# 480-column product blocks and a wider low matmul in a float32r AdaLN/LoRA feed-forward kernel

## The reference, cut to what matters

```python
# x: (8, 256, 1024) float32, ids: (8,) adapter numbers
y      = einsum('bsi,boi->bso', x, weight[ids])              # adapter, 1024 -> 1024
base   = y @ base_W.T + base_b                               # 1024 -> 1024
probs  = softmax(y @ router_W.T + router_b)                  # 15 routes
w      = sum over the 8 highest probs, by expert_map         # gate of each of 8 experts
h      = einsum('btd,erd->bter', y, A)                       # 8 experts x rank 16 = 128
out    = x + base + 2.0 * einsum('bter,eor->bto', h * w[..., None], B)
```

## Time and profile before

| | us |
|---|---|
| median of 3 runs | 404.02 |
| lowest, highest | 403.29, 405.07 |
| the profiled execution | 402.98 |
| its span, first to last instruction | 401.2 |

### The profile page before, as it was taken

One profiled execution on the slowest core, in us unless ns is written; L12 is line 12 of the kernel. 1 busy time (PEld: TensorE's weight loads), 2 busy tenths in 40 slices (PEclk: granted clock), 3 DMA queues, 4 the chain that ended last, 5 costly groups with the idle time before them and its releaser, 6 DMA issues.

```text
span 401.2 us, 5972 instructions
## 1 busy us (share of the span) xinstructions
PE 394.9 (98%) x2102; PEld 348.5 (87%) x2102; DVE 301.0 (75%) x561; ACT 157.7 (39%) x223; POOL 6.0 (1%) x13
## 2 busy tenths in 40 slices
PE   7999999999999999999999999999999999999996
PEld 6888888888888888889888888888888888888985
DVE  2769988878979884788758896589856899468763
ACT  3667344572145511554025630365304643144300
POOL 0000210000000000000000000000000000000000
PEclk9999999999999999999999999999999999999999
DMA  7999697830267305563066520775026830464002
GB/s 286 401 391 399 116 203 236 305 107 0 105 261 263 105 0 207 176 244 105 0 221 239 203 70 11 258 268 191 3 79 234 306 113 0 137 230 158 2 0 105
DMA packets 27277, 67.56 MB, mean 168 GB/s; under 512 B 3458, under 2 KB 14210, under 8 KB 27266
## 3 DMA queue, kind: packets, MB, share of 16 engines
q1 hardware_dynamic: 25106, 62.47, 43.9%
q0 software_dynamic: 1872, 3.90, 4.9%
q10 hardware_dynamic: 288, 1.05, 0.8%
HBM read 58.08 MB, written 8.39 MB: 166 GB/s over the span
## 4 chain that ended last, share of the span: by engine, by line
PE 93%; DMA 2%; DVE 2%; issue 1%; SPq 1%; ACT 0%; DVEq 0%
PE y_ps L823 27%; PE y_ps L825 14%; PE pl_ps L848 7%; PE x_ps L859 6%; PE x_ps L858 6%; PE x_ps L860 6%; PE s_ps L859 5%; PE s_ps L860 5%; PE s_ps L858 5%; PE pl_ps L849 4%; DMA w_raw<-in_wT 2%; PE y_ps L836 2%; PE s_ps L873 1%; PE s_ps L875 1%; PE s_ps L874 1%
## 5 line engine op out<-in xcount | busy, mean ns | idle before, releaser
L823 PE MATMUL y_ps<-x_split,w_hi 128*128 128x512 f32 x496 | 173.6, 394 | 0.3 <-DVE y_sum L529 0.3
L825 PE MATMUL y_ps<-x_split,w_lo 128*128 128x256 f32 x496 | 139.0, 280 | 0.0
L823 PEld LDWEIGHTS y_ps<-x_split,w_hi 128*128 128x128 f32 x496 | 92.9, 187 | 21.7 <-DVE w_lo L511 0.6
L825 PEld LDWEIGHTS y_ps<-x_split,w_lo 128*128 128x128 f32 x496 | 93.7, 189 | 0.4
L388 ACT CAST w_hi<-w_raw 128x1024 fp32r<-128x1024 f32 x58 | 60.8, 1049 | 75.8 <-DMA w_raw<-in_wT 75.5
L511 DVE TENSOR_TENSOR w_lo<-w_raw,w_hi 128x1024 fp32r<-128x1024 f32 x58 | 70.9, 1224 | 18.5 <-ACT w_hi L388 17.0
L380 ACT COPY y_sum<-y_ps 128x256 f32<-128x256 f32 x62 | 23.2, 374 | 66.6 <-PE y_ps L825 66.5
L848 PE MATMUL pl_ps<-pl_split,y_hi 128*128 128x480 f32 x128 | 42.7, 383 | 0.0
L529 DVE TENSOR_TENSOR y_sum<-y_ps,y_sum 128x256 f32<-128x256 f32 x62 | 26.1, 421 | 16.5 <-ACT y_sum L380 16.5
L849 PE MATMUL pl_ps<-pl_split,y_lo 128*128 128x240 f32 x128 | 34.9, 273 | 0.0
L858 PE MATMUL s_ps<-st_hi,y_hi 128*128 128x464 f32 x80 | 30.4, 380 | 0.0
(11 more groups left out here) (112 smaller groups left out, 543.3 us busy)
## 6 DMA issues: line engine op xcount, KB each, us to landing
w_raw<-in_wT SPq DMA_DIRECT2D x60, 512.0 KB, 3.4
res<-in_x SPq DMA_DIRECT2D x16, 512.0 KB, 4.7
x_raw<-in_xT SPq DMA_DIRECT2D x14, 512.0 KB, 4.8
out<-res SPq DMA_DIRECT2D x13, 512.0 KB, 3.4
early_raw<-in_wT SPq DMA_DIRECT2D x4, 512.0 KB, 8.5
hi_raw<-in_base_t SPq DMA_DIRECT2D x2, 928.0 KB, 10.5
st_raw<-in_base_t SPq DMA_DIRECT2D x2, 928.0 KB, 12.3
st_raw<-in_base_t POOLq DMA_DIRECT2D x2, 928.0 KB, 9.3
```

The costliest lines, as they stand in the source:

```text
L823: nc.tensor.matmul(y_ps[:, c % 2, :], w_hi[:, s, k, :], x_split[:, k, :, :].rearrange("p s t -> p (s t)"), start=(k == 0), stop=False)
L825: mm = nc.tensor.matmul(y_ps[:, c % 2, 0:T], w_lo[:, s, k, :], x_split[:, k, 0, :], start=False, stop=(k == KC - 1))
```

## The change

The number of plain columns goes from 96 to 64. With it NH goes from 464 to 480, PL from 240 to 208, HALF from 48 to 32, and the tiles that hold them follow. Line 848 becomes 2 x 208 = 416 wide. The low matmul of the plain part (line 849) would be 208 wide; it is made WL = 256 wide: it reads 208 high columns and the first 48 low columns of `pl_split[:, k]`, and so adds the product of the low part of `y` and the low part of the first 48 columns of A where high by low of these columns is summed. That is a term which the kernel before leaves out.

```diff
-    NP = 96
+    NP = 64
     NH = (D - NP) // 2
     PL = AR + NP
     DH = D // 2
     HALF = NP // 2
+    WL = 256
...
                         nc.tensor.matmul(pl_ps[:, t, 0:2 * PL], hi, pl_split[:, k, :, :].rearrange("p s n -> p (s n)"), start=(k == 0), stop=False)
-                        mm = nc.tensor.matmul(pl_ps[:, t, 0:PL], lo, pl_split[:, k, 0, :], start=False, stop=(k == KC - 1))
+                        mm = nc.tensor.matmul(pl_ps[:, t, 0:WL], lo, pl_split[:, k, :, :].rearrange("p s n -> p (s n)")[:, 0:WL],
+                                              start=False, stop=(k == KC - 1))
```

## The result

The changed kernel takes 407.87 us (median of 4 runs, 407.2 to 408.8) where the kernel before takes 403.65 us beside it: ratio 1.011, 95% interval 1.008 to 1.014. A second set of runs of the same changed kernel gave 407.25 against 403.27 us, 1.0096 (1.0079 to 1.0113). It is 4.0 to 4.2 us slower, and the forecast was 402.9 us with a range that ended at 406.8.

The account below looks back on a forecast made before the run. The prediction took the distances between TensorE's matmul starts to bound the kernel. Products +2.1, plain part -3.0, LoRA -0.2 and first stage 0 summed to -1.1 us, giving 402.9 us from a 404.02 us median, range 401.3 to 406.8 us.

Parts of the forecast that it names:

- What bounds the kernel: Whole run: TensorE, 98% busy at 2.4 GHz, sets the time as the sum of distances between 2,100 matmul starts.
- The price of 480: Block products: a 480-wide matmul costs its columns at 2.4 GHz plus 32 clock periods (13.3 ns), 213.3 ns.
- the other reading: Block products: 480 priced from its neighbour 464 with columns added and 3.5 ns kept, 216.9 ns; listed but not taken.
- Products: 684 block-product matmuls going from 464 to 480 columns, 3.1 ns more each: +2.1 us.
- Plain part: 128 pairs going from 480 and 240 to 416 and 256 columns, 23.3 ns less each: -3.0 us.
- LoRA: 96 matmuls of 512 columns, now preceded by a multiple of 32, at most 2.2 ns less each: -0.2 us.
- First stage: Unedited pairs of 512 and 256 columns in each element: 0 us if fast and slow stretches stay where they are.
- the cover that can fail: First stage's rhythm staying put: -0.9 us if the slow rhythm goes, +2.3 us if it spreads to the other 354 pairs.
- Covers: Work beside TensorE, such as conversions and y_lo, stays hidden at no cost; about 0.3 us left for B00 and y_lo.
- My balance of the loads: Transfers: block loads carry 32 KB more each, plain loads 64 KB less each, 128 KB against 128 KB.
- columns alone: Rival: no reward for multiples of 32; products +4.6 us, plain pairs -2.6 us, together +2.0 us, 406.0 us; chance 0.2.
- the spread of the slow rhythm: Rival: slow rhythm in all first stages (+2.3 us) and plain pairs (+0.8 us), total +2.0 us, 406.0 us; chance 0.12.

Follow-up runs that it names:

- the second changed execution: Second profiled execution of the unedited changed kernel, with no wait that the kernel before doesn't have: span 404.8 us, against 401.2 us before.
- the curve: Changed kernel with streams of 24 matmuls, 512 to 128 columns wide, behind its last element: 480 at 216.7 ns, 464 at 210.0 ns.
- the streams at like places: Changed kernel with 480 and 464 wide streams at varied start and bank columns behind its last element: 216.8 to 218.3 ns and 208.5 to 210.2 ns.
- those in the order of a product: Changed kernel with streams behind its last element turning high and low tiles as block products do: 464 at 209.0 ns, 480 at 216.8 ns.

## Why the prediction was wrong

The forecast moved the time by -1.1 us; the medians moved by +4.2 and +4.0 us, and the spans of the kernel before and of the second changed execution differ by +3.6 us. Term by term:

- *What bounds the kernel:* right. TensorE's starts are the time, before and after.
- *The price of 480, by the rule of columns plus 32 periods at multiples of 32:* the step that failed. I put 480 at 213.3 ns; streams of it give 216.7 to 218.3 ns, and the products 217.5. The rule rested on two widths, 512 and 256, which the curve shows to be two of the few that reach it. I had the other reading in the same list, 464 with its 3.5 ns kept, 216.9 ns for 480.
- *Products:* +2.1 us forecast, +5.2 measured. I had the step at 3.1 ns a matmul. The curve gives 6.7 ns, the streams at like places 7.7 to 8.1 ns, those in the order of a product 7.8 ns, and the products in the kernel grew by 7.6 ns on average (218.7 from 211.1 ns). 684 x 4.5 ns is the 3.1 us missed; why the step is 6.7 ns in one stream and 7.8 ns in another stays open.
- *Plain part:* -3.0 us forecast, -2.9 in the undisturbed execution. Right, because the pair of 416 and 256, 307.5 ns, lies 0.8 ns over the rule. Inside it the price of the widening was wrong: I counted 2.6 us of columns, the kernel without it shows 1.0.
- *LoRA:* -0.2 us forecast, 0.1 us more measured. No gain.
- *First stage:* the second step that failed. It stood at 0, with the rhythm named as the cover that can fail. It failed in elements 3 to 7 (+0.41 us each); element 1 turned fast (-0.41), and elements 0 and 2 are 0.35 us shorter together, mostly by a shorter wait: +1.3 us.
- *Covers:* y_lo had 0.3 us left by my count; 0.10 to 0.18 us were left where nothing came late. I had taken off the earlier TensorE and nothing for what stands ahead of y_lo: it ends 3.5 to 3.6 us behind the start of the plain part, 3.4 before. In two of seven profiles a late weight transfer used the rest up. The count was of one execution, where the weights were on time. My balance of the loads, 128 KB against 128 KB, left out the three accumulating transfers of GpSimd, whose blocks grow too; no run shows a cost of it.
- *The rivals:* columns alone was right in kind (+4.6 - 2.6 us, where +5.2 - 2.9 was measured), and the spread of the slow rhythm came in the same kernel, in the first stages but not in the plain pairs. I had given each its own 406 us and its own chance as if they excluded each other. They are two terms of one sum: with the 1.3 us that the first stages really cost, 404.0 + 2.0 + 1.3 = 407.3 us, beyond the end of the range.

## What to carry to other kernels

Before a width is changed for being a multiple of something, run a stream of each width in question: two widths that fit a rule are not a rule. Rivals that act on different terms must be added when the range is made, not weighed against each other. Where a matmul of this kind is at 240 columns or below and loads its weights each time, its columns are no longer what is paid, so columns should be moved into it and not out of it. A slack that is counted in one execution should be counted again in the changed one: here 0.3 us on paper were 0.1.

## What the runs showed of the hardware

- A float32r stream has a hump: over columns / 2.4 ns it costs 12.9 to 14.2 ns at 256 and 512 columns and, in its faster rhythm, at 496; 15.2 to 18.3 ns at 464 and 480. bf16 costs 2.7 to 2.8 ns.
- The same stream of float32r matmuls has more than one steady rhythm (346.7 or 353.3 ns for a pair of 512 and 256; 220.4 or 223.4 for 496), chosen by what TensorE ran just ahead. In this kernel it is worth 0.41 us per 64 pairs.
- From 240 columns down the distance stays at 110 to 112 ns, to the 128 of the last stream; each of these matmuls loads its weights.
